# Edge sweep of a graph network: segment sums split between VectorE and ScalarE, inverse root with one step fewer

## The chip, the cores and the metric

The kernel runs on one core of a Trainium2 chip. The metric is device time in microseconds (us) of one execution. Of the kernel before three runs are shown: 14583.35, 14586.31 and 14595.33 us, median 14586.31.

Engine names: TensorE is PE in the profile (its weight loads are PEld), VectorE is DVE, ScalarE is ACT, GpSimd is POOL, SyncE is SP.

## What is computed

Four graph layers follow each other on 6250 nodes and 206250 directed edges (sorted by destination), each followed by `x = layernorm(x + layer(x))`. The change touches the second, the only one with work for each edge. Cut to what matters, for each of its 4 heads:

```python
alpha = concat([q_i * K_v[src], q_i * K_E], axis=1) * scale      # q_i = K_v[dst], K_E = edge_feature @ Ke2v[h]
gate = sigmoid(_ln(alpha, ln_g[h], ln_b[h]))                     # _ln: (x - m) * rsqrt(v + eps) * g + b
m = concat([V_v[src], V_E], axis=1)
m = (m @ Wu[h] + bu[h]) * gate
m = _leaky(_ln(m @ Wm[h] + bm[h], mln_g[h], mln_b[h]))
heads.append(segment_sum(m, dst, num_segments=n))
```

## The kernel before

**Layout.** Edges are cut into 1616 tiles of 128 (`T`), four tiles make a group (`G`), so there are 404 groups (`NG`). `sweep1` is a software pipeline over the groups: each engine has its own instruction list with one body per step `i`, and in that body it works on several groups, each a fixed number of steps behind. The loop body on the chip holds four steps (`U`); the first 8 and the last few are written out (`steps`, L74). All hand-overs are semaphores that count; every engine takes its list strictly in order.

**What each engine does in step i.**

- POOL (L1301): the affine part of the message layer norm (`affine`, L1291, two operations on 128x1024, for the group whose scaled output `y` VectorE has just made), then eight indirect DMAs that gather the source rows (`table1`) and the destination's query rows (`table1q`) of a later group. The affine part waits for `chain2`, that is for VectorE's `y` (L743).
- VectorE (L653), in this order: `stats` of tiles 0 and 1 (eight bn_stats), `gate_m(0)` (L669), `stats` of tiles 2 and 3, `gate_m(1)`, the leaky relu that writes `msg` (L696), then the *chain*: `CH = 17` small operations (L715 to L735) on 16 or 32 columns that turn sums into an inverse root by a bit trick and three Newton steps of three operations each (L729, L731, L733), each waiting for the one before (`settle`); then `gate_m(2)`, `product` (L648, 128x2048), `y` (L743), `add(0)`, `add(1)`, `gate_m(3)`, `add(2)`, `add(3)`.
- ScalarE (L893), in this order: for the group of the step before, `norm` of head 1 (four activations, L904), `sigmoid(0)` (L910), `norm` of head 2, a copy of the turned node rows (L927), `sigmoid(1)`, `norm` of head 3, `sigmoid(2)`, `take_o(0)` (a square and a copy, L917 and L918), `sigmoid(3)`; then, once the chain of this step is done, `norm` of head 0 of group i, and `take_o(1)`. `gate_m(h)` waits for `sigmoid(h)`.
- PE (L1063): turns node rows (L1074), turns the four normalised heads (`turn`, L1081), `m_u` (L1089), `o_pair` (L1099, L1101), and `sums` (L1112).
- SP (L1411) issues the loads of kept keys, one-hot matrices and edge features.

**The sums.** Edges are sorted by destination, so the 128 edges of a tile fall into a window of 128 nodes that begins at the tile's first destination. `sums(j)` multiplies messages by a one-hot matrix into PSUM, banks 1 and 7, two tiles each, 128 columns for either half of the 256 features. `add(t)` (L673, its instruction is in the helper `add_tile`, L462 to L465) adds such a 128x256 block to `acc` in SBUF, at a column held in a register, and waits for the add before it, since windows overlap. The registers of four steps are loaded from memory at once by `block_bases` at the first step of the loop body (L658). The semaphore of these adds, `added1`, also tells PE when the PSUM bank is free again (L1108), and PE and SP that the sweep is over (L1142, L1427).

```python
def add_tile(added, g, t, at_, sums):
    after(dve, added, g * G + t)
    V.tensor_tensor(at_, at_, sums, ALU.add).then_inc(added, 1)
```

After the sweep come the rest of this layer and two more layers, and ahead of it stand the building of an adjacency matrix and the first layer; none of that is touched.

## Time and profile before

| what | value |
|---|---|
| runs | 14583.35, 14586.31, 14595.33 us |
| the profiled execution | 14678.36 us, its span 14676.6 us |
| busy in the span: PE, PEld, DVE, ACT, POOL | 74%, 48%, 62%, 38%, 56% |
| mean granted clock of TensorE | 0.881 of full speed |

The profile is of one execution. An engine's busy time leaves out its waits and its register, branch and semaphore instructions. A row of instructions by time gives the start, the time taken, engine, line, operation, names, count, and in brackets how long the engine had been idle and what ended that. Idle time marked "issue" ended by nothing that the profile shows, "remote" by an event whose sender it does not name. A row of a time window gives for each engine the busy time and, in brackets, the number of instructions.

### The profile page before, as it was taken

To read this page: it belongs to the slowest core of one execution; us is meant where nothing else is said; L and a number is where in the kernel's file an instruction comes from. 1 tells how busy PE (TensorE), PEld (TensorE's weight loads), DVE (VectorE), ACT (ScalarE), POOL (GpSimd) and SP (SyncE) were. 2 spreads that over 40 slices of the span, in tenths; PEclk is the share of its full clock that TensorE was granted. 3 is DMA by queue.
4 is the path that set the end of the run, shared out by engine and by line. 5 is a ranking of instruction groups with operands and counts; after the bars stand their busy time and mean duration, and the time that the engine had idled before them with its cause. 6 is when DMAs were issued, how large, how long until landed. Compare 5 with 4: busy or idle time off the path is not lost.

```text
span 14676.6 us, 179769 instructions
## 1 busy us (share of the span) xinstructions
PE 10837.4 (74%) x44178; PEld 7098.1 (48%) x44178; DVE 9067.6 (62%) x21076; ACT 5510.9 (38%) x11343; POOL 8172.4 (56%) x6219
## 2 busy tenths in 40 slices
PE   0444444444968888888888888888888888999997
PEld 0333333332436655656556556655565633554443
DVE  2333333332048889888888888899889822666333
ACT  0111111111016666666666666666666500000332
POOL 1588888887017777777777777677777600000000
PEclk9999999999978889888888888899888888555998
DMA  9666666666843333333333333333333365443443
GB/s 418 172 160 150 152 152 150 150 155 154 306 162 118 111 110 119 115 115 114 113 113 116 112 112 113 114 119 120 115 114 117 92 219 215 158 154 144 152 153 103
DMA packets 1156188, 2147.06 MB, mean 146 GB/s; under 512 B 344859, under 2 KB 767133, under 8 KB 1104606
## 3 DMA queue, kind: packets, MB, share of 16 engines
q1 hardware_dynamic: 765822, 1661.13, 33.9%
q0 software_dynamic: 390240, 484.27, 14.5%
q8 instruction: 76, 1.25, 0.0%
q14 instruction: 50, 0.41, 0.0%
HBM read 1652.06 MB, written 492.83 MB: 146 GB/s over the span
## 4 chain that ended last, share of the span: by engine, by line
PE 37%; issue 12%; ACT 12%; POOL 11%; another core or an unknown queue 10%; DVE 9%; DMA 5%; SPq 3%; DVEq 1%; ACTq 0%; POOLq 0%
POOL adj L1282 11%; PE psum L1042 7%; PE psum L1170 7%; ACT arena L904 7%; PE psum L1099 5%; PE psum L1201 4%; PE psum L1190 4%; PE psum L1081 3%; DMA adj<-put_val,put_idx 3%; PE psum L1089 3%; SPq L1331 2%; PE psum L1112 2%; DVE arena L663 2%; ACT arena L910 1%
## 5 line engine op out<-in xcount | busy, mean ns | idle before, releaser
L1282 POOL DMA_INDIRECT adj<-put_val,put_idx x1616 | 2638.5, 1633 | 882.2 <-issue 462.1
L904 ACT ACTIVATE arena<-arena 128x128 f32<-128x128 f32 x6464 | 2672.2, 492 | 190.6 <-DVE arena L735 88.0
L1025 PE MATMUL psum<-ke,arena 64*128 64x256 f32 x3232 | 1451.6, 640 | 1658.7 <-DMA arena<-in_edge_t 1658.7
L1099 PEld LDWEIGHTS psum<-wm,arena 128*128 128x128 f32 x12928 | 1830.3, 213 | 1004.7 <-issue 510.8
L1099 PE MATMUL psum<-wm,arena 128*128 128x64 f32 x12928 | 1925.4, 298 | 402.3 <-ACT arena L918 322.7
L1243 POOL DMA_INDIRECT arena<-table1q,idx_dst x1616 | 1809.4, 1120 | 498.6 <-issue 498.6
L910 ACT ACTIVATE arena<-psum,cols 128x512 f32<-128x512 f32 x1616 | 1257.3, 778 | 2150.3 <-remote 1538.2
L1025 PEld LDWEIGHTS psum<-ke,arena 64*128 64x128 f32 x3232 | 1041.5, 330 | 2068.3 <-issue 1796.0
L1243 POOL DMA_INDIRECT arena<-table,idx_blk x1616 | 1704.5, 1055 | 433.3 <-issue 375.7
L1089 PE MATMUL psum<-arena,wvu 128*128 128x512 f32 x3232 | 1907.5, 675 | 16.4 <-DVE arena L669 11.1
L1081 PE MATMUL psum<-ident,arena 128*128 128x128 f32 x6464 | 1195.4, 314 | 631.3 <-ACT arena L904 603.5
L882 ACT ACTIVATE arena<-psum 128x512 f32<-128x512 f32 x808 | 483.3, 598 | 2961.7 <-PE psum L1025 2684.1
L1295 POOL TENSOR_TENSOR arena<-arena,mg 128x1024 f32<-128x1024 f32 x404 | 951.6, 2355 | 1001.8 <-DVE arena L743 998.5
L669 DVE SCALAR_TENSOR_TENSOR arena<-psum,cols,arena 128x512 f32<-128x512 f32 x1616 | 1204.1, 745 | 378.5 <-ACT arena L910 298.5
L663 DVE BATCH_NORM_STATS2 arena<-arena 128x6 f32<-128x128 f32 x6464 | 1321.9, 278 | 139.1 <-issue 138.8
L1081 PEld LDWEIGHTS psum<-ident,arena 128*128 128x128 f32 x6464 | 848.1, 160 | 1134.8 <-ACT arena L904 697.5
L1112 PE MATMUL psum<-arena 128*128 128x128 f32 x6464 | 1096.2, 314 | 266.8 <-issue 152.0
L572 DVE TENSOR_TENSOR arena<-arena 128x1024 f32<-128x1024 f32 x202 | 247.7, 1226 | 1609.3 <-DMA arena<-key_lin 1609.3
L1112 PEld LDWEIGHTS psum<-arena 128*128 128x128 f32 x6464 | 936.2, 216 | 631.6 <-issue 590.5
L1042 PE MATMUL psum<-arena 128*64 128x392 f32 x3136 | 1037.9, 494 | 70.5 <-DMA arena<-adj 67.3
L1170 PE MATMUL psum<-acc,arena 65*128 65x392 f32 x1568 | 1024.8, 861 | 15.3 <-DVE acc L796 15.3
L1298 POOL TENSOR_TENSOR arena<-arena,mb 128x1024 f32<-128x1024 f32 x404 | 951.0, 2354 | 31.7
(188 smaller groups left out, 13171.3 us busy)
## 6 DMA issues: line engine op xcount, KB each, us to landing
arena<-adj SPq DMA_DIRECT2D x294, 1568.0 KB, 6.1
kept_keys<-arena SPq DMA_DIRECT2D x404, 512.0 KB
arena<-kept_keys SPq DMA_DIRECT2D x404, 512.0 KB
adj<-arena SPq DMA_DIRECT2D x98, 1568.0 KB
arena<-adj SPq DMA_DIRECT2D x196, 784.0 KB, 4.2
arena<-key_lin SPq DMA_DIRECT2D x202, 512.0 KB
arena<-in_edge_t SPq DMA_DIRECT2D x808, 128.0 KB
kept_hot<-arena SPq DMA_DIRECT2D x404, 256.0 KB
```

What stands on the lines that cost most here:

```text
L663: V.bn_stats(st[:, t * H + h, :], halves(pair[s][:, :, D:PAIR])[:, t, :, h * D:(h + 1) * D]).then_inc(stats1, 1)
L904: A.activation(to, at_, ACT.Identity, bias=shift[z][:, n:n + 1], scale=rstd[z][:, n:n + 1]).then_inc(normed, 1)
L910: A.activation(gate[:, h % 2, :], psum[:, 2 + h % 2, :], ACT.Sigmoid, bias=cols[:, 2, h:h + 1], scale=cols[:, 1, h:h + 1]).then_inc(gated, 1)
L1025: last = M.matmul(psum[:, 2 + 2 * z + j, t * H * D:(t + 1) * H * D], edge0[z][:, 2 * j + t, :], ke[D:P, :], start=True, stop=True)
L1042: last = M.matmul(psum[0:D, i, 0:CH_N], xa[:, c, :], blk[n % SLOTS][:, i * CH_N:(i + 1) * CH_N], start=c == 0, stop=c == NC - 1)
L1081: last = M.transpose(psum[:, 2 + h % 2, t * P:(t + 1) * P], normal[h % 2][:, t, :], ident[:, :])
L1089: M.matmul(psum[:, 4 + h % 2, :], wvu[:, h, :], xt[prev].rearrange("p t n -> p (t n)"), start=True, stop=True).then_inc(m_done, 1)
L1099: M.matmul(psum[:, 6, at_ + h * D:at_ + (h + 1) * D], gm[z][:, h, 2 * j + t, :], wm[:, h, :], start=h == 0, stop=False)
L1112: last = M.matmul(psum[:, 1 + 6 * j, at_:at_ + WIN], msg[z][:, t * H + 2 * half:t * H + 2 * half + 2, :].rearrange("p h d -> p (h d)"), on ...
L1170: last = M.matmul(psum[:, 4 * b + i, 0:CH_N], nh_b[:, c, :], nh_t[:, q * GRP + i * CH_N:q * GRP + (i + 1) * CH_N], start=True, stop=True)
L1243: K.indirect_dma_start(out=dst[:, t, :], out_offset=None, in_=table, in_offset=bass.IndirectOffsetOnAxis(ap=idx[:, t:t + 1], axis=0)).then ...
L1282: K.indirect_dma_start(out=adj, out_offset=bass.IndirectOffsetOnAxis(ap=put_idx[s][:, j:j + 1], axis=0), in_=put_val[s][:, j:j + 1], in_of ...
```

## The change

In the edge sweep `add(t)` goes. The sums of a group are taken in one step later (five behind, not four). VectorE's `carry(t)` adds only one column of `acc`, the first of the window, for both halves (128x2 elements), to the block in PSUM; ScalarE's `window(t)` then copies the whole 128x256 block from PSUM over `acc` at the register's column. `carry(t)` waits for the copy of the tile before (`copied`), `window(t)` for its carry (`carried`). The carries stand at four places of VectorE's first half of a step, the copies at four places of ScalarE's list. PE, and the ends of the sweep on PE, VectorE and SP, wait for `copied` in place of `added1`; SP's load after the sweep also waits for the end of the chain. ScalarE now loads the base registers too. In the chain the three Newton steps (nine operations) become one third-order step of four and one Newton step of three: `CH` goes from 17 to 15.

```diff
-        added1 = sem("added1")
+        carried = sem("carried")
+        copied = sem("copied")
-        CH = 17
+        CH = 15
...
-                now = [inside or 0 <= i - lag < NG for lag in range(5)]
+                now = [inside or 0 <= i - lag < NG for lag in range(6)]
                 z, odd = s % 2, (s + 1) % 2
-                if now[4] and s == 0:
-                    held[:] = block_bases(DVE, i - 4)
+                if inside and s == 0:
+                    held[:] = block_bases(DVE, i - 5)
                 regs = held[G * s:G * s + G]
+                if now[5] and not inside:
+                    regs = bases(DVE, dst_t[0:1, (i - 5) * G:(i - 4) * G])
...
-                def add(t):
-                    if now[4]:
-                        dve.wait_ge(sums1, 2 * (i - 4) + t // 2 + 1)
-                        add_tile(added1, i - 4, t, acc[:, :, bass.ds(regs[t], WIN)],
-                                 psum[:, 1 + 6 * (t // 2), (t % 2) * 2 * WIN:(t % 2 + 1) * 2 * WIN].rearrange(
-                                     "p (j w) -> p j w", j=2))
-
+                def carry(t):
+                    if now[5]:
+                        dve.wait_ge(sums1, 2 * (i - 5) + t // 2 + 1)
+                        after(dve, copied, G * (i - 5) + t)
+                        first = psum[:, 1 + 6 * (t // 2), (t % 2) * 2 * WIN:(t % 2 + 1) * 2 * WIN].rearrange(
+                            "p (j w) -> p j w", j=2)[:, :, 0:1]
+                        V.tensor_tensor(first, first, acc[:, :, bass.ds(regs[t], 1)], ALU.add).then_inc(carried, 1)
+
+                carry(0)
                 if now[0]:
                     after(dve, chain1, i * CH)
                     dve.wait_ge(products, i + 1)
                     stats(0)
                     stats(1)
+                carry(1)
                 if now[1]:
                     after(dve, o_done, 2 * (i - 2))
                     gate_m(0)
+                carry(2)
                 if now[0]:
                     stats(2)
                     stats(3)
                 if now[1]:
                     gate_m(1)
+                carry(3)
...
-                for scale in (1.0, 1.0, P ** 0.5):
-                    settle()
-                    small_step(V.scalar_tensor_tensor(u, root, -0.5 * scale, root, ALU.mult, ALU.mult))
-                    settle()
-                    small_step(V.tensor_tensor(u, u, var, ALU.mult))
-                    settle()
-                    small_step(V.scalar_tensor_tensor(root, u, 1.5 * scale, root, ALU.add, ALU.mult))
+                settle()
+                small_step(V.scalar_tensor_tensor(u, root, 1.0, root, ALU.mult, ALU.mult))
+                settle()
+                small_step(V.tensor_tensor(u, u, var, ALU.mult))
+                settle()
+                small_step(V.scalar_tensor_tensor(u, u, -10.0 / 3.0, u, ALU.add, ALU.mult))
+                settle()
+                small_step(V.scalar_tensor_tensor(root, u, 5.0, root, ALU.add, ALU.mult))
+                settle()
+                small_step(V.scalar_tensor_tensor(u, root, -0.5 * 0.375 ** 3 * P ** 0.5, root, ALU.mult, ALU.mult))
+                settle()
+                small_step(V.tensor_tensor(u, u, var, ALU.mult))
+                settle()
+                small_step(V.scalar_tensor_tensor(root, u, 1.5 * 0.375 * P ** 0.5, root, ALU.add, ALU.mult))
...
-                add(0)
-                add(1)
                 if now[1]:
                     gate_m(3)
-                add(2)
-                add(3)
             product(0, 0)
-            steps(dve, sweep1, NG, 8, 4, spare=U)
-            dve.wait_ge(added1, T)
+            steps(dve, sweep1, NG, 8, 5, spare=U)
+            dve.wait_ge(copied, T)
...
+            held = []
+
             def sweep1(i, k, s, inside):
 
-                now = [inside or 0 <= i - lag < NG for lag in range(3)]
+                now = [inside or 0 <= i - lag < NG for lag in range(6)]
                 z, odd = s % 2, (s + 1) % 2
+                if inside and s == 0:
+                    held[:] = block_bases(ACT_E, i - 5)
+                regs = held[G * s:G * s + G]
+                if now[5] and not inside:
+                    regs = bases(ACT_E, dst_t[0:1, (i - 5) * G:(i - 4) * G])
+
+                def window(t):
+                    if now[5]:
+                        act.wait_ge(carried, G * (i - 5) + t + 1)
+                        A.activation(acc[:, :, bass.ds(regs[t], WIN)],
+                                     psum[:, 1 + 6 * (t // 2), (t % 2) * 2 * WIN:(t % 2 + 1) * 2 * WIN].rearrange(
+                                         "p (j w) -> p j w", j=2), ACT.Copy).then_inc(copied, 1)
...
                 if now[1]:
                     norm(i - 1, (s + 3) % U, odd, 1)
+                window(0)
+                if now[1]:
                     sigmoid(0)
                     norm(i - 1, (s + 3) % U, odd, 2)
+                window(1)
                 if now[0]:
...
                 if now[1]:
                     sigmoid(1)
+                window(2)
+                if now[1]:
                     norm(i - 1, (s + 3) % U, odd, 3)
                     sigmoid(2)
+                window(3)
...
-            steps(act, sweep1, NG, 4, 2)
+            steps(act, sweep1, NG, 8, 5, spare=U)
...
-                    after(pe, added1, G * (i - 5) + 2 * j + 2)
+                    after(pe, copied, G * (i - 5) + 2 * j + 2)
...
-            pe.wait_ge(added1, T)
+            pe.wait_ge(copied, T)
...
-            sp.wait_ge(added1, T)
+            sp.wait_ge(copied, T)
+            sp.wait_ge(chain1, CH * (NG + 5))
```

## Rows read from the trace of the kernel before

**Rows 1.** The page: the span, and busy time with share and count by engine.
```profile
span 14676.6 us, 179769 instructions
...
PE 10837.4 (74%) x44178; PEld 7098.1 (48%) x44178; DVE 9067.6 (62%) x21076; ACT 5510.9 (38%) x11343; POOL 8172.4 (56%) x6219
```

**Rows 2.** Busy time by window, the stretch of the edge sweep.
```profile
4340.00:11700.00 7360.00, 6032.01 (x32084) 4402.97 (x32084) 6396.65 (x17664) 4648.90 (x10048) 5433.34 (x4501) 0.86 0.38 114
```

**Rows 3.** `product`, one a step: count, durations, first and last start.
```profile
L648 DVE TENSOR_TENSOR arena<-arena x404: 2274/2281/2327, 4315.3 to 11689.2; 128x2048 f32<-128x2048 f32 x135
```

**Rows 4.** Busy time by window, four single steps, from `product` to `product`.
```profile
7479.04:7495.71 16.67, 13.27 (x83) 9.60 (x83) 15.96 (x45) 11.62 (x26) 11.11 (x10) 1.00 0.34 110
7495.71:7512.38 16.67, 13.16 (x53) 9.33 (x52) 15.83 (x45) 10.39 (x23) 13.92 (x12) 0.65 0.38 119
8042.79:8061.09 18.30, 15.31 (x77) 10.96 (x78) 16.05 (x45) 11.50 (x25) 13.21 (x13) 0.81 0.36 115
7512.38:7534.13 21.75, 15.69 (x91) 11.46 (x90) 16.12 (x45) 11.30 (x25) 15.34 (x13) 0.89 0.37 115
```

**Rows 5.** Groups of instructions, 6000 to 9000 us: busy us, mean ns, idle before.
```profile
L904 ACT ACTIVATE arena<-arena 128x128 f32<-128x128 f32 x2599 | 1074.4, 492 | 65.2 <-DVE arena L735 35.7 <-issue 14.0 <-DVE arena L731 11.4
...
L910 ACT ACTIVATE arena<-psum,cols 128x512 f32<-128x512 f32 x649 | 505.0, 778 | 883.4 <-remote 638.4 <-PE psum L1081 187.7 <-issue 56.8
...
L465 DVE TENSOR_TENSOR acc<-acc,psum 128x256 f32 x648 | 271.1, 418 | 117.0 <-PE psum L1112 67.5 <-DVE acc L465 15.0 <-remote 2.3
...
L918 ACT ACTIVATE arena<-psum 128x512 f32<-128x512 f32 x324 | 192.0, 593 | 0.0
...
L717 DVE SCALAR_TENSOR_TENSOR arena<-arena 128x16 f32<-128x16 f32 x163 | 29.5, 181 | 0.0
```

**Rows 6.** VectorE by time, step 7495.71 to 7512.38.
```profile
7497.91 1.22 DVE L743 TENSOR_TENSOR arena<-arena 128x1024 f32<-128x1024 f32 x1
...
7503.68 1.64 DVE L663 BATCH_NORM_STATS2 arena<-arena 128x6 f32<-128x128 f32 x8
7505.37 0.75 DVE L669 SCALAR_TENSOR_TENSOR arena<-psum,cols,arena 128x512 f32<-128x512 f32 x1
...
7511.01 0.19 DVE L731 TENSOR_TENSOR arena<-arena 128x32 f32<-128x32 f32 x1
7511.24 0.19 DVE L733 SCALAR_TENSOR_TENSOR arena<-arena 128x32 f32<-128x32 f32 x1
7511.47 0.18 DVE L735 SCALAR_TENSOR_TENSOR arena<-arena 128x16 f32<-128x16 f32 x1
```

**Rows 7.** ScalarE by time, the same step.
```profile
7499.28 0.60 ACT L917 ACTIVATE arena<-psum 128x512 f32<-128x512 f32 x1 [2.47 <-remote]
...
7500.26 1.65 ACT L904 ACTIVATE arena<-arena 128x128 f32<-128x128 f32 x4
7501.81 0.77 ACT L910 ACTIVATE arena<-psum,cols 128x512 f32<-128x512 f32 x1
7502.47 1.65 ACT L904 ACTIVATE arena<-arena 128x128 f32<-128x128 f32 x4
...
7504.50 0.78 ACT L910 ACTIVATE arena<-psum,cols 128x512 f32<-128x512 f32 x1
```

**Rows 8.** GpSimd, PE and ScalarE by time, a step of 18.3 us, one row each.
```profile
8046.29 2.35 POOL L1295 TENSOR_TENSOR arena<-arena,mg 128x1024 f32<-128x1024 f32 x1 [2.73 <-DVE arena L743]
...
8057.98 0.60 PE L1081 MATMUL psum<-ident,arena 128*128 128x128 f32 x4
...
8063.18 0.78 ACT L910 ACTIVATE arena<-psum,cols 128x512 f32<-128x512 f32 x1 [4.15 <-remote]
```

**Rows 9.** VectorE by time, the same step of 18.3 us.
```profile
8044.99 1.22 DVE L743 TENSOR_TENSOR arena<-arena 128x1024 f32<-128x1024 f32 x1
...
8050.18 1.64 DVE L663 BATCH_NORM_STATS2 arena<-arena 128x6 f32<-128x128 f32 x8 [1.41 <-issue]
```

**Rows 10.** ScalarE by time, a step of 21.75 us.
```profile
7532.57 0.78 ACT L910 ACTIVATE arena<-psum,cols 128x512 f32<-128x512 f32 x1 [6.80 <-remote]
```

More of the change, by code:

```diff
@@ L24 @@
 DVE = mybir.EngineType.DVE
+ACT_E = mybir.EngineType.Activation
 PE = mybir.EngineType.PE
@@ L460, in one_hot @@
                     iota_f[:, :].unsqueeze(1).to_broadcast([P, G, WIN]), ALU.is_equal)
-            def add_tile(added, g, t, at_, sums):
-                after(dve, added, g * G + t)
-                V.tensor_tensor(at_, at_, sums, ALU.add).then_inc(added, 1)
             link(V.memset(zeros, 0.0), mark="zeros")
```

## The prediction

> **What bounds the kernel now.** I read the page first: no engine is near full over the span, which only says that stages differ [rows 1]. The busy times by window come next: the edge sweep takes half of the time, and in it VectorE is busy for 6397 of 7360 us, PE for 6032, ScalarE for 4649 [rows 2]. That is an average over different steps, so I cut the sweep into steps. `product` runs once a step, 404 times, from 4315.3 to 11689.2 us: 18.3 us a step [rows 3]. The 403 intervals between its starts fall into three kinds: 154 under 17.3 us (mean 16.6), 145 from 17.3 to 19 (mean 18.0), 104 above (mean 21.1); one step or two of each kind stand in [rows 4].
>
> What do engines wait for in a step? The groups by line show little before VectorE's adds (117 us in some 162 steps, 0.72 a step) and the greatest waits before ScalarE's sigmoid: 883 us, 5.5 a step, 638 of it ended by an event with no named sender [rows 5]. Single steps show what that does [rows 4]:
>
> - *Short steps, 16.67 us.* VectorE is busy 15.8 to 16.0 us; with the handing over inside its chain nothing is left: VectorE alone sets these.
> - *Middle steps, 18.3 us.* VectorE's own work is the same, and 1.6 us are waits.
> - *Long steps, 21.75 us.* A sigmoid is held for 6.8 us, and VectorE behind it.
>
> ScalarE's part in a short step: `norm` of head 1 starts at 7500.26, `sigmoid(1)` at 7504.50, `gate_m(1)` on VectorE at 7505.37, and the chain's last operation starts at 7511.47 [rows 6, 7]. So gate and chain hang on ScalarE's list with hardly any slack, though VectorE never stood still. That round (ScalarE's norms and sigmoids, then gate, `msg` and chain, then the next norm of head 0) is the second bound, right under the first.
>
> The third is the held event. PE's turn of head 3 is in the trace at 8057.98 (0.60 us), and the sigmoid that waits for it starts at 8063.18 [rows 8]. I can't say what holds it, but when it comes free is regular: 16.8 to 17.0 us after the end of VectorE's `y` in the step before. With y's end 3.42 us after the start of `product` (7499.13 against 7495.71) [rows 4, 6], it is 7482.46 to 7499.28 [rows 7], 8046.21 to 8063.18 [rows 8, 9], and 7515.80 to 7532.57 [rows 4, 10]. GpSimd starts its work for a group at the end of `y` (8046.29) [rows 8], and its affine part and eight gathers fill that time, so I take the event to be tied to GpSimd's list.
>
> **The change, part by part.**
>
> *VectorE's own work.* Four adds of 0.42 us go [rows 5]. Four additions on 128x2 come. No row has that size: the nearest is the 128x16 operation, 0.18 us [rows 5], a PSUM operand and a register column may add a little, so I take 0.20; the ends are 0.10 (when it overlaps its neighbours) and 0.42 (the add itself). Saved: 4 x 0.22 = 0.88 us. The chain loses two of its operations, each 0.23 us from start to start (7511.01, 7511.24, 7511.47) [rows 6]: 0.46 us. Together 1.34 us, VectorE's list becomes 15.3 us long. The third-order step's two new operations are of the kinds of those they replace.
>
> Here a rule of the Trainium skill can be weighed (page "VectorE: DVE Perf Modes", section on the TRN2 errata). It says that an operation pays a fixed latency whatever its size, and gives 120 cycles plus one for each element from PSUM, 0.13 us for a carry. The 0.18 us for 16 elements [rows 5] agree with a fixed part, not with so low a figure. An estimate by that page would make the sum below some 45 us smaller.
>
> *ScalarE's list.* Four copies of 128x256 out of PSUM come. A sigmoid of 512 columns takes 0.778 us, a norm of 128 0.492: 0.745 ns a column. The copy of 512 takes 0.593, so one of 256 takes 0.40 [rows 5]. A square and a copy take 0.98 us together (7499.28 to 7500.26) [rows 7], 0.49 each where they last 0.59, so neighbours overlap by 0.10 and a copy adds 0.30 to the list (ends 0.28 and 0.49). ScalarE is busy 10.4 to 11.6 us a step [rows 4], so 1.2 us more doesn't fill it. But two of the copies lie in the round.
>
> *The hand-overs.* This is the part that costs. `carry(2)` waits for `copied` of tile 1, and behind `carry(2)` VectorE has `stats` of tiles 2 and 3, `gate_m(1)`, and all the rest. The copy of tile 1 stands behind `norm` of head 2. Before, those stats ran beside `norm` of head 2 (7503.68 beside 7502.47) [rows 6, 7]. From the start of `norm` 1: 1.55 (norm) + 0.30 (copy) + 0.66 (sigmoid) + 1.55 (norm) + 0.40 (copy) + 0.10 (hand-over, as from `y` to GpSimd at 8046.21 to 8046.29 [rows 8, 9]) + 0.20 (carry) + 1.69 (stats, 7503.68 to 7505.37) = 6.45 us to `gate_m(1)`, against 5.11 before: +1.34. Then `carry(3)` +0.20 and the chain -0.46. The round gets longer by 1.08 us. `carry(0)`, `carry(1)` and the other two copies cost nothing here: the carry before `gate_m(0)` waits for a copy that stands ahead of the sigmoid which that gate needs anyway. If ScalarE came earlier, they would cost 0.2 each on VectorE.
>
> *What of it shows.* In a middle step the held event frees ScalarE, the round follows, `y` ends 4 us after the chain, and the event after next comes 16.9 us after that `y`. The loop spans two steps and has one round in it, so a step grows by 0.54: 145 x 0.54 = +78 us. In a long step the event, one sigmoid, `gate_m(2)`, `product`, `y` and 16.9 us make 21.7 us; neither chain nor copies are in it. I take half of the 104 as such and half as steps after them, with 0.54: +28 us. Short steps come mostly in pairs, one without a held event, which gains VectorE's 1.34, and one in which the event, 1.34 earlier with `y`, is followed by a round 1.08 longer: 77 x (1.08 - 1.34) = -20 us.
>
> *Registers.* VectorE's load of the base registers stops it for 1.41 us once in four steps [rows 9]; that stays. ScalarE gets the same at the head of its body. It can go on behind `take_o(1)` (0.98 us), which leaves 0.43 x 101 = +43 us; ends 0 and 142.
>
> *Edges of the sweep.* One more step at the end, with four hand-overs and a chain: +8 us. The waits of PE and SP for `copied` come a step later than the adds, but PE's `sums(0)` stands behind the turn and product of head 2, later than the copy of tile 1; nothing. SP's wait for the chain holds only the load of the node rows, hidden behind the work on the sums.
>
> Sum: 78 + 28 - 20 + 43 + 8 = +137 us, on the profiled execution's 14678.36. That lies 92 us (0.6%) above the median of the runs; the sweep is in both, so I add to the median: **14720 us**.
>
> **The rivals.**
>
> *Faster: VectorE is the bound and the hand-overs hide.* For it speaks that VectorE is the busiest engine of the sweep and sets 154 steps alone. Then these win 1.34 each (206 us), and the others half of the 0.72 us wait before the adds, which goes since the sums are a step old: 249 x 0.36 = 90. It would be 14290 us. It decides for this side if the copy of tile 1 ends by the time that `gate_m(0)` ends; the rows of the short step have it 1.8 us later. Chance 0.36.
>
> *No change:* the copies cost what the chain and adds bring, most likely if carries and copies are at their low ends. Chance 0.14.
>
> *Slower by much: more long steps.* Longer ScalarE lists put the turn of head 2 behind the point where events are held. If 146 more steps went from 17.3 to 21.75 us, it would be +650, 15240 us. Against it: the turn of head 2 waits for PE's own work ahead of it too. Chance 0.07.
>
> *The change doesn't do what it says:* if `copied` had no reader on VectorE the ordering cost would be missing; the diff shows the wait, so this has no share.
>
> **How the numbers follow.** The forecast has 0.43. Its own range, with carries, copies and registers at their ends, is 14600 to 14950. The range reaches down to the faster case, 14280, and up to 14960; what lies outside is the rival of long steps and a gain for every step of VectorE's whole 1.34 us. A measurement of this kernel can tell about 0.2%, 29 us, from no change. Faster by more: 0.37; within: 0.13; slower by more: 0.50.
>
> **What would show it.** In the profile after: the carry near 0.2 us and the copy near 0.40; VectorE busy some 1.2 us less a step; idle time before the carry of tile 2 ended by ScalarE's copy, 1 us or more a step; waits before the sigmoids no smaller; the held event still 16.9 us after `y`. I am wrong if VectorE waits for no copy, if short steps fall to 15.3 us with nothing added in the others, or if the three kinds of step change their shares: the sum takes these as given, its weakest point.

## The result, and the profile after

The change makes the kernel faster on the chip of this comparison: 14375.9 us (median of four runs, 14359.58 to 14379.67) against 14584.8 (four runs, 14466.37 to 14595.33), ratio 0.988 with an interval of 0.984 to 0.991. I had forecast 14720. The profiled execution took 14374.66 us, against 14678.36 before. The page of the kernel after, its span, busy time and granted clock:

```profile
span 14372.9 us, 183141 instructions
...
PE 10467.0 (73%) x44178; PEld 6905.9 (48%) x44178; DVE 8445.1 (59%) x20275; ACT 5951.8 (41%) x12960; POOL 8787.5 (61%) x6219
...
PEclk9999999999988999999999999999999898555998
```

Against [rows 1] VectorE has lost 622 us of busy time, ScalarE has gained 441. The engine that the change doesn't touch has gained too: GpSimd, 615 us on the same 6219 instructions. `product`'s row, which answers to [rows 3]:

```profile
L645 DVE TENSOR_TENSOR arena<-arena x404: 2276/2281/2291, 4326.8 to 11383.7; 128x2048 f32<-128x2048 f32 x135
```

From the first to the last start it is 7056.9 us instead of 7373.9. These 317 us are the whole difference of the spans (304), so only the sweep counts. Cut into steps it looks like another kernel. Before, 154 intervals were short (mean 16.6), 145 middle (18.0) and 104 long (21.1). After, by the same bounds, 14 are short, 385 middle (mean 17.5, and 380 of them within 0.15 us of 17.52) and 4 long; seven of these 18 stand at the start of the sweep. The fast steps are all but gone, and so are the long ones. The groups of instructions from 6000 to 9000 us (busy us, mean ns, idle before), some 171 steps:

```profile
L1270 POOL DMA_INDIRECT arena<-table1q,idx_dst x684 | 941.3, 1376 | 208.4 <-issue 208.4
L1270 POOL DMA_INDIRECT arena<-table,idx_blk x685 | 767.3, 1120 | 182.8 <-issue 159.1 <-POOL idx_dst L1333 19.9
L1322 POOL TENSOR_TENSOR arena<-arena,mg 128x1024 f32<-128x1024 f32 x171 | 404.6, 2366 | 9.5 <-DVE arena L754 6.6
...
L700 DVE SCALAR_TENSOR_TENSOR arena<-arena 128x1024 f32<-128x1024 f32 x171 | 209.4, 1225 | 242.6 <-POOL arena L1325 242.6
...
L678 DVE TENSOR_TENSOR psum<-psum,acc 128x2 f32<-128x2 f32 x684 | 109.0, 159 | 199.0 <-ACT acc L915 99.6 <-issue 98.9
...
L931 ACT ACTIVATE arena<-psum,cols 128x512 f32<-128x512 f32 x684 | 530.9, 776 | 506.8 <-PE psum L1108 354.4 <-issue 136.0 <-remote 16.4
L915 ACT ACTIVATE acc<-psum 128x256 f32 x684 | 258.5, 378 | 1.3 <-DVE psum L678 0.3
...
L1139 PE MATMUL psum<-arena 128*128 128x128 f32 x2736 | 462.4, 320 | 487.1 <-DVE arena L700 484.7 <-ACT acc L915 1.4 <-issue 1.0
```

Read them from the sigmoid (L931). The waits that a remote event ended were 638 us [rows 5] and are 16. VectorE waits for ScalarE's copies: 99.6 us before the carries (L678), and nearly all of the 98.9 us called "issue" is the same wait. Of the 171 carries of tile 2, 80 have a wait that ends with the copy of tile 1 and 91 have one of the same length, 1.03 us in the mean, for which the trace shows no event. But VectorE's largest wait stands before `msg` (L700), 242.6 us, and that is for GpSimd's second affine operation (L1325). GpSimd itself waits for `y` (L754) 9.5 us in 171 steps. An engine that waits for nobody, and for which the others wait, sets the pace. The chain of waits says so too; GpSimd had 11% of it before:

```profile
POOL 38%; PE 27%; issue 18%; DMA 4%; ACT 4%; DVE 4%; SPq 3%; POOLq 1%; another core or an unknown queue 0%; ACTq 0%; DVEq 0%
```

One step by time, of the kernel after (start, duration, engine and line; in brackets the idle time and what ended it):

```profile
8000.61 2.28 DVE L645 TENSOR_TENSOR arena<-arena 128x2048 f32<-128x2048 f32 x1
...
8000.98 2.74 POOL L1270 DMA_INDIRECT arena<-table1q,idx_dst  x1 [0.30 <-issue]
...
8003.42 1.64 ACT L925 ACTIVATE arena<-arena 128x128 f32<-128x128 f32 x4
...
8004.02 0.95 POOL L1270 DMA_INDIRECT arena<-table1q,idx_dst  x1 [0.30 <-issue]
...
8007.48 2.37 POOL L1322 TENSOR_TENSOR arena<-arena,mg 128x1024 f32<-128x1024 f32 x1
...
8009.55 0.73 DVE L668 SCALAR_TENSOR_TENSOR arena<-psum,cols,arena 128x512 f32<-128x512 f32 x1
...
8012.31 1.23 DVE L700 SCALAR_TENSOR_TENSOR arena<-arena 128x1024 f32<-128x1024 f32 x1 [1.96 <-POOL arena L1325]
8012.56 1.85 POOL L1270 DMA_INDIRECT arena<-table,idx_blk  x1 [0.15 <-POOL idx_dst L1333]
...
8018.13 2.28 DVE L645 TENSOR_TENSOR arena<-arena 128x2048 f32<-128x2048 f32 x1
...
8025.00 2.37 POOL L1322 TENSOR_TENSOR arena<-arena,mg 128x1024 f32<-128x1024 f32 x1
```

GpSimd's list takes 17.52 us from L1322 to L1322, `product` to `product` is 17.52 too. A gather that meets no wide VectorE operation takes 0.95 us; the one that runs under `product` takes 2.74, and the one under `msg` 1.85. How long depends on where it starts: all 170 gathers from 6000 to 9000 us that start inside `product` end 0.82 us after it, here 8003.72 against 8002.89. Those that start inside `msg` end 0.88 us after it. `msg` waits 1.96 us for the affine part. I call such a step *locked* below, and a sigmoid that waits for an event with no named sender *held*.

### The profile page after: what moved, and what is told of

Same layout as the page of the kernel before. It is cut to its first block, busy times and chain, and to the rows that moved or that the text cites. A ratio compares the mean times of both kernels' runs of the same rounds, so it can differ in the third digit from the quotient of the medians.

```text
span 14372.9 us, 183141 instructions
## 1 busy us (share of the span) xinstructions
PE 10467.0 (73%) x44178; PEld 6905.9 (48%) x44178; DVE 8445.1 (59%) x20275; ACT 5951.8 (41%) x12960; POOL 8787.5 (61%) x6219
## 4 chain that ended last, share of the span: by engine, by line
POOL 38%; PE 27%; issue 18%; DMA 4%; ACT 4%; DVE 4%; SPq 3%; POOLq 1%; another core or an unknown queue 0%; ACTq 0%; DVEq 0%
POOL arena L1270 19%; POOL adj L1309 11%; PE psum L1069 7%; PE psum L1197 7%; POOL arena L1322 5%; PE psum L1228 4%; PE psum L1217 4%; DMA adj<-put_val,put_idx 3%; SPq L1358 2%; ACT arena L925 2%; POOL arena L1325 2%; PE psum L1126 1%; POOL idx_dst L1333 1%; PE psum L1139 1%; DMA arena<-key_lin 1%
## 5 line engine op out<-in xcount | busy, mean ns | idle before, releaser
L1270 POOL DMA_INDIRECT arena<-table1q,idx_dst x1616 | 2219.4, 1373 | 492.3 <-issue 492.3
L1270 POOL DMA_INDIRECT arena<-table,idx_blk x1616 | 1812.9, 1122 | 431.7 <-issue 375.9
L1126 PEld LDWEIGHTS psum<-wm,arena 128*128 128x128 f32 x12928 | 1741.9, 202 | 606.0 <-issue 508.4
L1116 PE MATMUL psum<-arena,wvu 128*128 128x512 f32 x3232 | 1849.1, 657 | 0.0
L1126 PE MATMUL psum<-wm,arena 128*128 128x64 f32 x12928 | 1786.2, 284 | 10.1 <-issue 9.6
L931 ACT ACTIVATE arena<-psum,cols 128x512 f32<-128x512 f32 x1616 | 1254.4, 776 | 1189.7 <-PE psum L1108 831.5
L1108 PE MATMUL psum<-ident,arena 128*128 128x128 f32 x6464 | 1139.1, 304 | 246.1 <-ACT arena L925 213.9
L1108 PEld LDWEIGHTS psum<-ident,arena 128*128 128x128 f32 x6464 | 818.4, 155 | 618.6 <-ACT arena L925 484.3
L1322 POOL TENSOR_TENSOR arena<-arena,mg 128x1024 f32<-128x1024 f32 x404 | 956.0, 2366 | 72.3 <-DVE arena L754 65.7
L1325 POOL TENSOR_TENSOR arena<-arena,mb 128x1024 f32<-128x1024 f32 x404 | 948.3, 2347 | 31.7
```

The lines of the kernel that those rows point to most:

```text
L1108: last = M.transpose(psum[:, 2 + h % 2, t * P:(t + 1) * P], normal[h % 2][:, t, :], ident[:, :])
L1116: M.matmul(psum[:, 4 + h % 2, :], wvu[:, h, :], xt[prev].rearrange("p t n -> p (t n)"), start=True, stop=True).then_inc(m_done, 1)
L1126: M.matmul(psum[:, 6, at_ + h * D:at_ + (h + 1) * D], gm[z][:, h, 2 * j + t, :], wm[:, h, :], start=h == 0, stop=False)
L1270: K.indirect_dma_start(out=dst[:, t, :], out_offset=None, in_=table, in_offset=bass.IndirectOffsetOnAxis(ap=idx[:, t:t + 1], axis=0)).then ...
L1322: K.tensor_tensor(y4, y4, mg[:, :].unsqueeze(1).to_broadcast([P, G, H * D]), ALU.mult).then_inc(y_affine, 1)
```

## The experiments

Eighteen runs, on five further chips. The time of the kernel before turned out to go with the chip, so its time stands beside each; chips are lettered, A is that of the comparison. Without `mb` (both), after + 0.72 us on C and the file of before again on F are single executions, all others medians of four or more.

| chip | kernel before | other kernels on it |
|---|---|---|
| A | 14584.8 | after 14375.9 |
| B | 14698.5 | short chain alone 14372.1; split alone 14890.0; without `mb`: after 15144.3, before 15160.8 |
| C | 14112.7 | after with a late carry 14355.5; before + 0.72 us of GpSimd 14729.5; after + the same 14547.0; after, half of `mb` on VectorE 13987.2 |
| D | 14516.9 | the same file again 14521.8; after 14361.2; short chain alone 14374.0; short chain, half of `mb` on VectorE 14253.2 |
| E | 14566.6 | after 14373.4; before + 0.36 us of GpSimd 14397.4; split alone + 0.72 us 14668.5; after, half of `mb` on VectorE 14477.2 |
| F | 14111.3 | the same file again 14115.4; short chain, half of `mb` on VectorE 14238.0 |

The first eight expectations use letters where they don't spell a theory out: A, VectorE's list sets the pace before and GpSimd's after; B, what changed is the mix of step kinds; C, my forecast's round; D, the lock, that is, all steps fall into one kind once GpSimd never waits.

**The two halves of the change apart.** The short chain in the kernel before:

```diff
-        CH = 17
+        CH = 15
-                for scale in (1.0, 1.0, P ** 0.5):
-                    ...
+                small_step(V.scalar_tensor_tensor(u, u, -10.0 / 3.0, u, ALU.add, ALU.mult))
+                ...
```

> The kernel before with the shorter chain alone (CH 15), adds left on VectorE. Theory A (in the kernel before VectorE's list sets the pace; after the change GpSimd's list of 17.5 us a step does): VectorE's list goes from 16.7 to 16.2 us, so short steps fall by 0.46 us, 154 x 0.46 = 71 us, and the long ones stay: about 14510. Theory B (the mix of step kinds is what matters, and any change of phase can end the long steps of 20 to 22 us): the long steps vanish here too and the time is at or below the changed kernel's, 14200 to 14400. Theory C (my prediction's round of ScalarE and VectorE): 0.46 less in the round, 0.23 a step: about 14490.

14372.1 us on chip B, ratio 0.977 (0.975 to 0.980). 396 steps of 17.56 us; from 6000 to 9000 us:

```profile
L917 ACT ACTIVATE arena<-psum,cols 128x512 f32<-128x512 f32 x684 | 528.7, 773 | 726.2 <-PE psum L1088 463.2 <-issue 248.7 <-DVE arena L669 14.2
...
L696 DVE SCALAR_TENSOR_TENSOR arena<-arena 128x1024 f32<-128x1024 f32 x170 | 208.4, 1226 | 184.2 <-POOL arena L1305 184.2
...
L1302 POOL TENSOR_TENSOR arena<-arena,mg 128x1024 f32<-128x1024 f32 x171 | 404.7, 2367 | 2.9
```

No held sigmoid, `msg` behind GpSimd, GpSimd never waiting: two small operations fewer are enough for the lock. The split with the long chain (`CH = 17` and the three Newton steps back in the kernel after):

> The changed kernel with the three Newton steps put back (CH 17). Theory A: GpSimd's list sets 17.52 us a step and VectorE has slack, so the chain's 0.46 us cost nothing: same as the changed kernel, 14375 within 30, and steps of 17.5 us. Theory C: the round is 0.46 longer, 0.23 to 0.46 a step, 14470 to 14560.

14890.0 us, ratio 1.014 (1.011 to 1.017), with 79, 207 and 117 steps of 16.6, 18.2 and 20.9 us:

```profile
L924 ACT ACTIVATE arena<-psum,cols 128x512 f32<-128x512 f32 x643 | 502.3, 781 | 745.2 <-remote 557.4 <-PE psum L1101 152.8 <-issue 34.5
...
L678 DVE TENSOR_TENSOR psum<-psum,acc 128x2 f32<-128x2 f32 x644 | 106.8, 166 | 372.7 <-ACT acc L908 354.9 <-issue 16.9 <-PE psum L1132 0.8
...
L1315 POOL TENSOR_TENSOR arena<-arena,mg 128x1024 f32<-128x1024 f32 x161 | 379.3, 2356 | 465.6 <-DVE arena L747 464.7 <-issue 0.8
```

Here is much of what I had forecast for the change: carries that wait 355 us for ScalarE's copies, middle steps longer (18.24 against 18.04), +1.4%. But the shares have moved here too, short steps from 154 on A to 79, so the 1.4% aren't the costed terms alone; the kernel before wasn't profiled on B. Alone the split costs. On chip D both locked kernels ran side by side:

> The changed kernel, beside the others of this call. Theory of the locked step: 14355 to 14385 us whatever the chip, nearly all steps 17.5 us, no sigmoid that waits for an event it should have had. Its ratio to the kernel before then goes with the chip alone: 1.017 where before takes 14113 us, 0.986 where it takes 14585, 0.978 where it takes 14699. Rival, a gain that belongs to the change: 0.988 again on any chip.

> Before with the short chain of small steps alone, beside the changed kernel on one chip. Theory that the short chain is the whole gain: within 0.2% of the changed kernel (14355 to 14385 us), steps of 17.5 to 17.6 us. Rival, the carried sums' split has its own part: the changed kernel differs from it by over 0.3%, to either side.

14361.2 and 14374.0 us, 0.1% apart. With the short chain the split adds nothing worth the name. The ratio of the change there, 0.990 (0.987 to 0.993), is set by the kernel before.

**Does the order of carry and copy bind after the change?** `carry(2)` behind the moments of tiles 2 and 3:

```diff
-                carry(2)
                 if now[0]:
                     stats(2)
                     stats(3)
+                carry(2)
```

> The changed kernel with the carry of tile 2 moved behind the bn_stats of tiles 2 and 3, so that they no longer wait for ScalarE's copy of tile 1. Theory A (GpSimd's list sets a fixed 17.52 us a step): nothing changes, 14375 within 30. Theory C (the order of carry and copy lengthens the round and the round counts): 0.3 to 0.6 us a step less, 14130 to 14250.

Steps of 17.54 us as in the kernel after, 14355.5 us. The wait of the carries goes (199.0 us in all to 24.9). About half of it reappears before `msg`, for GpSimd (242.6 to 329.8), and as much before the gates, for the sigmoids (some 23 to 118 us). The round is there, but it hides under GpSimd's list.

**GpSimd's list, shorter.** Both kernels without the addition of `mb`, so without one 2.35 us operation of GpSimd (the affine part then lacks its shift):

```diff
-                K.tensor_tensor(y4, y4, mb[:, :].unsqueeze(1).to_broadcast([P, G, H * D]),
-                                ALU.add).then_inc(y_affine, 1)
```

> The changed kernel without the second of GpSimd's two affine operations (the addition of mb, 2.35 us a step); the layer norm's shift is left out. Theory A: a step falls by up to 2.35 us until the next bound, ScalarE's and VectorE's round, takes over: 15.4 to 16.2 us a step, 13550 to 13850 in all. Theory C (round is the bound already): steps stay at 17.5 us, 14375.

> The kernel before without the addition of mb on GpSimd. If the event that holds a sigmoid comes free by GpSimd's list (16.9 us after y's end), it now comes 14.5 us after y's end, the waits before the sigmoid with no named sender shrink from 638 us in the window 6000 to 9000 to under 200, and steps go to 16.7 us, VectorE's list: about 13950. If it is tied to something else, waits and step kinds stay: 14550 to 14600.

The event 14.5 us after `y` came, but both forecasts of the time missed: the kernels are slower by far, 15144 and 15161 us, with 393 and 388 of the 403 steps at 19.5 and 19.6. By time, before without `mb`:

```profile
8012.07 0.78 ACT L910 ACTIVATE arena<-psum,cols 128x512 f32<-128x512 f32 x1 [7.10 <-remote]
...
8013.63 2.28 DVE L648 TENSOR_TENSOR arena<-arena 128x2048 f32<-128x2048 f32 x1
...
8015.83 1.22 DVE L743 TENSOR_TENSOR arena<-arena 128x1024 f32<-128x1024 f32 x1
...
8017.13 2.36 POOL L1295 TENSOR_TENSOR arena<-arena,mg 128x1024 f32<-128x1024 f32 x1 [6.60 <-DVE arena L743]
...
8031.56 0.78 ACT L910 ACTIVATE arena<-psum,cols 128x512 f32<-128x512 f32 x1 [4.43 <-PE psum L1081]
```

Now nearly every step is a long one: the sigmoid starts 14.5 us after the end of `y` (8017.05 to 8031.56). From 4500 to 11300 us 345 of 347 steps have a wait of over 2 us that ends 14.1 to 14.9 us after `y` (the trace names TensorE's turn for 110 of them, as in the last row, and no sender for the others), 14.53 in the median. In the kernel before, 177 of 371 steps have one, and it ends 16.9 us after `y`. The event comes earlier by the 2.35 us of the operation taken out. The kernels further down agree, on other chips: with half of the addition off GpSimd (1.08 us less) the median is 15.7, with 0.36 us more 17.1, and in the split alone it goes from 16.9 to 17.4 with 0.72 us more. That the held event is tied to GpSimd's list, which I had only supposed, is shown by this. But less work on GpSimd gave more held events, not fewer.

**GpSimd's list, longer.** A useless addition on 128x256 (0.72 us) or 128x84 (0.36 us) behind the affine part:

```diff
+                K.tensor_tensor(pad[:, :], mg[:, :], mb[:, :], ALU.add)
```

> The kernel before with one useless addition of 128x256 more a step on GpSimd, behind the affine part (estimated 0.6 us, a quarter of the 2.35 us of 128x1024). Theory D (lock): the kernel before is slow since VectorE's y comes just after GpSimd has run out of work, GpSimd waits for it, and its gathers then fall where they hold PE's events; if GpSimd's list is made longer than VectorE's, GpSimd never waits, all steps fall into one kind and the kernel becomes faster: steps of 17.4 to 17.9 us, 14350 to 14550, though work was added. Simple theory (more work on a busy engine costs): 14600 to 14950.

> The changed kernel with the same useless addition. GpSimd's list sets the pace there: the step grows by the addition's own time, 0.6 us, from 17.52 to some 18.1 us, 14600 to 14640. If VectorE's and ScalarE's round sets it: 14375.

On chip C before locks, at 18.47 us, but gains nothing by it: 14729.5 us, ratio 1.044 (1.042 to 1.045) where 14350 to 14550 us were expected. After stays locked, at 18.01, which is 0.48 more than the late carry's 17.53 there and less than the addition's 0.73; the eight gathers, placed otherwise against VectorE's list, take 9.07 us a step instead of 10.03. Half of it in the kernel before, on chip E, and the whole in the split alone:

> Before with a useless addition of 84 columns on GpSimd, some 0.36 us by the 0.72 us of 256 columns and the 2.35 us of 1024. With 0.72 us the steps locked at 18.5 us, with nothing they mix. Theory: GpSimd's list is then about 17.9 us; if that is longer than the round the steps lock at 17.9 to 18.1 us and the time is 14500 to 14580 us; if not, they mix with a mean over 18.1 us and the time is that of before or above it. The first has my larger chance, 0.6.

> The split with the long chain (14890 us, mixed steps) and a useless 0.72 us addition more on GpSimd. Theory, the steps lock where GpSimd's list is longer than the round: nearly all steps between 18.0 and 18.5 us, no sigmoid that waits for a late event, 14550 to 14740 us, so faster than without the addition. Rival, the long chain itself makes the mix: three kinds of steps as before and over 14890 us.

Neither locked. The split keeps three kinds (44, 306 and 53 steps); its ratio is 1.006 (1.004 to 1.008) on E, that of the split without the addition was 1.014 on B. So "a list longer than the round locks" falls as a rule, and the lock of the padded kernel before on chip C may be that chip's. But the kernel before with 0.36 us of useless work more takes 14397.4 us, ratio 0.988 (0.986 to 0.990), beside 0.986 (0.984 to 0.988) for the change on the same chip. It has 183, 203 and 17 steps of the three kinds, and fewer held waits than the kernel before in either of its profiles with such waits, 638 us on A and 416 on D (on E it has no profile):

```profile
L911 ACT ACTIVATE arena<-psum,cols 128x512 f32<-128x512 f32 x684 | 530.3, 775 | 655.3 <-remote 317.9 <-PE psum L1082 267.8 <-issue 67.9
```

Nearly the gain of the change, with nothing saved on any engine. What brings it is, as far as these profiles can be compared, that the long steps go: 17, against 104 on A and 77 on D.

> The changed kernel again, for the same chip as the others of this call: 14350 to 14385 us, as on three chips so far, steps of 17.5 us, whatever before takes here.

14373.4 us there. On three chips the changed kernel takes 14361 to 14376 us.

**Why the kernel before differs by chip.** Its own file again, on D and on F:

> The kernel before, unchanged, for a profile on the chip on which the others of this call run. Theory: its time hangs on the mix of step lengths, so it should be anywhere from 14110 to 14730 us (what its runs on three chips gave), with the mean step of the sweep between 16.6 and 18.4 us and, in every step over 17.3 us, a sigmoid that waits for TensorE's event; if it comes out at 14110 us, three steps in four or more should be short (16.2 to 17.3 us). Rival: on a fast chip every instruction is shorter; then the product and the moments would take less than the 3.9 and 2.2 us of the profile of before.

> The kernel before, once more, for its profile. Theory that its time is set by how many of TensorE's events come late to the sigmoid: the idle time that the sigmoid shows with a remote releaser in 6000 to 9000 us is about 640 us at 14680 us and about 430 us at 14510 us, and near nothing if this is a chip on which it takes 14110 us. Rival: the same idle time at any total.

On D 14521.8 us, with 190, 136 and 77 steps of the three kinds, on F 14115.4. Its rows on F, the groups from 6000 to 9000 us:

```profile
L910 ACT ACTIVATE arena<-psum,cols 128x512 f32<-128x512 f32 x710 | 548.8, 773 | 648.5 <-PE psum L1081 607.9 <-DVE arena L669 39.0
...
L1243 POOL DMA_INDIRECT arena<-table1q,idx_dst x710 | 816.2, 1150 | 216.3 <-issue 216.3
L1243 POOL DMA_INDIRECT arena<-table,idx_blk x708 | 725.9, 1025 | 189.0 <-issue 163.5 <-POOL idx_dst L1306 19.1
L1295 POOL TENSOR_TENSOR arena<-arena,mg 128x1024 f32<-128x1024 f32 x178 | 419.6, 2357 | 176.0 <-DVE arena L743 176.0
```

and a step by time on F:

```profile
8013.57 2.28 DVE L648 TENSOR_TENSOR arena<-arena 128x2048 f32<-128x2048 f32 x1
...
8014.63 2.04 POOL L1243 DMA_INDIRECT arena<-table1q,idx_dst  x1 [0.30 <-issue]
...
8015.77 1.22 DVE L743 TENSOR_TENSOR arena<-arena 128x1024 f32<-128x1024 f32 x1
...
8017.07 2.37 POOL L1295 TENSOR_TENSOR arena<-arena,mg 128x1024 f32<-128x1024 f32 x1 [0.40 <-DVE arena L743]
...
8030.06 2.28 DVE L648 TENSOR_TENSOR arena<-arena 128x2048 f32<-128x2048 f32 x1
```

Not one wait of the sigmoid is ended by a remote event, and the steps follow a strict pattern: three of 16.5 us and one of 18.1, the one in which VectorE loads its registers. The instructions are as long as on A (`product` 2281 ns, affine 2357), so it is no chip with shorter instructions (`product` takes 2.28 us in every profile, not the 3.9 of the expectation of the first of these runs); it is the same kernel without held events. Held waits from 6000 to 9000 us go with the time: 638 us at 14678 us [rows 5], 416 on D at 14513, none on F at 14115.

What differs between the chips can be narrowed down. On C and F no sigmoid of any kernel, six profiles of six kernels, waits for an event with no named sender. The traces also list each update of a semaphore, and in these six TensorE's turns from 6000 to 9000 us all have theirs, or all but one (709 of 710 for the kernel before on F). In all fourteen profiles on A, B, D and E some are missing: 609 for 649 turns in the kernel before on A, and 555 for 684 in the locked kernel after on the same chip. So the disturbance is the chip's, it is there in the locked kernels too, and what the lock changes is that no sigmoid waits on it for long. Nor is it the turn alone: in the step of [rows 8] the events of `sums`, `turn`, `m_u` and `o_pair` all come between 8063.10 and 8063.37, after more than 5 us without one (the last before is at 8058.00). In 96 of the 114 unnamed sigmoid waits over 2.5 us from 6000 to 9000 us, two to four of these four kinds come together like that.

Against this clean step the locked one is the slower: 17.52 against a mean of 16.9. GpSimd's own rows say why. On F its list has 16.08 us and a wait of 0.40; after the change the gather that meets `product` starts 0.37 us behind it instead of 1.06, and so takes 2.74 us instead of 2.04, another meets the whole of `msg` (1.85 us) and not its end, and by the means of the groups the eight gathers of a step take 4 x (1.376 + 1.120) = 9.98 us instead of 4 x (1.150 + 1.025) = 8.70. The copy of their indices, which falls under `msg` in 40 of 171 steps and then takes 1.22 us, takes 0.44 in the mean instead of 0.18. The 0.40 us of waiting are used up too.

**A version that beats both?** Half of the `mb` addition moved to VectorE ahead of `msg`, in the kernel after:

```diff
+                    yh = y[z].rearrange("p (t h) d -> p t (h d)", t=G)[:, 2:4, :]
+                    V.tensor_tensor(yh, yh, mb[:, :].unsqueeze(1).to_broadcast([P, 2, H * D]),
+                                    ALU.add).then_inc(shifted, 1)
...
-                K.tensor_tensor(y4, y4, mb[:, :].unsqueeze(1).to_broadcast([P, G, H * D]),
+                K.tensor_tensor(y4[:, 0:2, :], y4[:, 0:2, :], mb[:, :].unsqueeze(1).to_broadcast([P, 2, H * D]),
```

> The changed kernel with half of the addition of mb (tiles 2 and 3 of a group) moved from GpSimd to VectorE: GpSimd's list loses 1.17 us, VectorE's gains 0.69 (15.3 to 16.0). If the lock holds with so small a margin: steps of 16.4 to 16.9 us, 13930 to 14130. If VectorE's y then comes after GpSimd is free, the steps mix again: 14500 to 14900.

> The changed kernel with half of the mb addition on VectorE, again, beside before and the changed kernel on one chip. Theory: 13970 to 14000 us as on the other chip, since most of its steps don't hang on the mix: 2.6 to 2.8% under the changed kernel. Rival, the first was a lucky chip: above 14100 us here.

On C it took 13987.2 us, 0.991 (0.989 to 0.993) of a kernel before at its best, with 367 steps between 16.1 and 17.3 us, 16.5 in the mean. On E it took 14477.2, 0.7% over the changed kernel there, and its six executions spread from 14349 to 14536 us; the profile is of the fastest. The sigmoid's row on C, and then on E:

```profile
L937 ACT ACTIVATE arena<-psum,cols 128x512 f32<-128x512 f32 x722 | 560.7, 777 | 374.3 <-PE psum L1114 374.3
```

```profile
L937 ACT ACTIVATE arena<-psum,cols 128x512 f32<-128x512 f32 x683 | 533.9, 782 | 760.5 <-remote 633.9 <-PE psum L1114 78.8 <-issue 47.6
```

The held events are back on E: the lucky-chip rival was right. The same move with the wide adds kept:

> Before with the short chain alone, and with the addition of mb to tiles 2 and 3 moved from GpSimd to VectorE (an instruction of some 0.4 us there before msg; GpSimd's list about 1.0 us shorter). Theory that GpSimd's list alone sets the locked step: 16.5 us steps as with the same move in the changed kernel, 13950 to 14030 us. Rival, VectorE's list, which still has the four wide additions here (0.42 us each instead of 0.16): it becomes the bound at 17.0 us or more and gives 14150 us or more. Third: the steps fall out of the lock and mix (means of 17.8 us or more, 14400 us and up).

> Before with the short chain, and half of the mb addition on VectorE, again. Theory that no event comes late in it, so that it has one time on all chips: 14240 to 14270 us, three steps of 16.8 us and one of 18.7 us in turn. Rival, it goes with the chip as the version with the split does (13987 and 14477 us): off by more than 0.5% from 14253 us.

14253.2 us on D, 0.8% under the changed kernel (14361.2) and 0.983 (0.977 to 0.988) of before, and 14238.0 on F, which is 1.009 (1.007 to 1.011) of before there. Three steps of 16.78 us and one of 18.67 on both: its mean of 17.25 is the VectorE-bound rival of its expectation, where I had put 16.5. It beats both kernels on a chip with held events and loses to before on one without. The expectation of the second run gave a reason that doesn't hold: the sigmoid's held waits are 182 us on D and none on F, and the two times still agree within 0.1%. So not every held wait costs time; the half-shifted kernel on E had 634 us of them in a run of 14349 us. No version here beats both everywhere.

## Why the prediction was wrong

The parts that I costed came out nearly as put:

- *Carry, copy, chain.* The carry takes 0.159 us (put at 0.20), the copy 0.378 (0.40) and adds 0.26 to ScalarE's list (8004.96 to 8005.22; put at 0.30). VectorE's busy time in the steps from 6000 to 9000 us falls from 15.9 to 14.4 us; I had 1.34 us less. My estimate of 0.13 us by the table in the Trainium skill (page "VectorE: DVE Perf Modes", section on the TRN2 errata) is 0.03 us off, my 0.20 is 0.04 off; neither matters.
- *The round.* `norm` of head 1 starts at 8003.42, `gate_m(1)` at 8009.55: 6.13 us, against 5.11 before and the 6.45 forecast. It did get longer, for the reason given, and the wait before the carry of tile 2 is the 1 us a step that I named as a sign: 83.4 us with the copy named and 93.9 without, in 171 steps. In the split alone this adds to the time; in the change it doesn't, because the 1.96 us before `msg` cover it.
- *Registers.* ScalarE's load shows as a stop of 0.49 us before `norm` of head 1, 42 times in 171 steps, close to the 0.43 that I left it. VectorE's, 1.41 us once in four steps before, no longer stops it at all. Both lie under GpSimd's list, so the +43 us weren't there. The +8 us for the edges of the sweep no run tells apart.

The step that failed is the one named as the weakest: that the three kinds of step keep their shares. They went from 154, 145 and 104 to 14, 385 and 4. That term was put at zero; the sum had +137 us, and the sweep came out 317 us shorter. Two of the signs that I named say the same: the waits before the sigmoids fell from 883 to 507 us, and no event came 16.9 us after `y` any more. Two things stood under it. I had tied the held event to GpSimd's list and then costed nothing on GpSimd; its gathers, stretched by VectorE's wide operations, became the bound at 17.52 us, and no rival had that. And I took 16.9 us from `y` to the event as a fixed part of the kernel, not as something that a slightly earlier chain can do away with.

The "faster" rival had the direction and nearly the size (14290), but not the mechanism. It had VectorE's saving show in each step; the steps that VectorE set alone went from 16.6 to 17.5, and the saving was spent in waits for GpSimd. The gain came from the long steps, and the split, which the rival counted on, had no part in it. One reading in its condition was off as well: by the terms of my own sum the copy of tile 1 would end at 7504.72 in the short step, and `gate_m(0)` is over when the moments behind it start, at 7503.68 [rows 6]: 1.0 us, not 1.8.

A wider doubt belongs to the result itself. "1.2% faster" holds on A, D and E (ratios 0.988, 0.990, 0.986). On C and F the kernel before takes 14111 to 14113 us, and the late-carry version, whose steps are those of the kernel after, took 14355.5 on C: 1.7% slower. The kernel after itself wasn't tried on C or F; that the change loses there is what the numbers say, not a run.

**What stays open.** What holds TensorE's events, and why two of six chips don't show it. The granted clock doesn't explain it: the half-shifted kernel on E had 0.920 in the mean and 634 us of held waits, the kernel before on F 0.916 and none. It isn't settled either what decides for the lock: with GpSimd's list as it is, a chain of 15 locked on all five chips where it ran, 0.36 us more of GpSimd's work in the kernel before did not. That gathers are held by VectorE's wide operations is read from where they start and end in several kernels; it wasn't tried alone.

## What to carry to other kernels

When steps of a pipeline differ although they do the same work, ask first what makes the kinds and whether a small shift in time can change their shares; a sum per step with fixed shares can have the wrong sign. Cost each engine's whole list, the ones that the change leaves alone too, with their durations as they are when they meet other work. And run a kernel with such a mix on several chips before calling a per cent or two a gain.

## What the hardware showed that I had not expected

- Useless work made the kernel faster: 0.36 us more on GpSimd in each step, 1.2% less time on a chip with held events. On a chip without them 0.72 us more cost 4.4%.
- One kernel, the same durations of its instructions in the three profiles of it (A, D and F), and six chips: 14111, 14113, 14517, 14567, 14585 and 14699 us. The locked kernels without added work agree within 0.15% on all five chips where they ran (14356 to 14376).
- GpSimd's indirect DMA instruction takes 0.95 us by itself. One that starts inside `product` ends 0.82 us after it, whenever it started (170 of them in the kernel after, 133 in the kernel before on F), so it takes 2.04 or 2.74 us; inside `msg` it takes 1.85. Both are VectorE operations with two inputs from SBUF. `product` keeps its 2281 ns, but `msg` takes 1.70 and 1.73 us instead of 1.22 in the two kernels on C with the useless addition of 0.72 us.
- Events of TensorE that come several at once, some 4.6 us after the turn's place in the trace (8058.58 to 8063.18 [rows 8]), at a time that follows GpSimd's list, and only on four of six chips.
